# Attention in a ViT tower: the softmax reciprocals spread through DRAM instead of by matmuls, with normalisation and output projection placed later

## What is computed

```
h = concat(cls_tok, edge(x))                       # 32 x 257 x 256
q, k, v = split(layernorm(h) @ w_qkv + b_qkv)      # 16 heads of 16
att = softmax(causal(q @ k.T / 4))
y   = att @ v                                      # heads side by side: 32 x 257 x 256
h   = h + y @ w_out + b_out
h   = h + ffn(layernorm(h))                        # quantised with one scale over all tokens
```

## Time and profile before

| | |
|---|---|
| median of 3 runs | 1192.98 us (1190.79 to 1196.33) |
| the profiled execution: its time | 1186.23 us |
| its span, first to last instruction | 1184.5 us |
| TensorE matmul busy | 960.0 us, 81% |
| VectorE busy | 829.9 us, 70% |
| ScalarE busy | 702.2 us, 59% |
| GpSimd busy | 556.7 us, 47% |
| mean granted TensorE clock | 0.954 of full, 1.00 in the steady part of the attention block |

### The profile page before, as it was taken

How to read it: one execution, slowest core, us unless ns; L and a number is a source line. 1 busy time by engine, 2 the same in 40 slices (tenths; PEclk the granted TensorE clock), 3 DMA queues, 4 the chain that set the end, 5 groups by cost and what they waited for, 6 DMA issues and landing times. The chain is left out here.

```text
span 1184.5 us, 28089 instructions
## 1 busy us (share of the span) xinstructions
PE 960.0 (81%) x9574; PEld 690.6 (58%) x9584; DVE 829.9 (70%) x1967; ACT 702.2 (59%) x1187; POOL 556.7 (47%) x702
## 2 busy tenths in 40 slices
PE   2277899889899989999998989999987478885565
PEld 1055666667676767667676766777765244333343
DVE  1825566777767777776777776767665369998998
ACT  0154556666666666666666666666543167776796
POOL 5233555665566565565556556556543254430000
PEclk9988899999999999999999999999997689997889
DMA  3854555555545655555565555554330024203863
GB/s 88 229 132 114 132 144 135 143 144 149 131 128 148 155 136 149 145 125 136 151 149 140 152 133 128 139 137 116 89 79 13 6 96 194 103 1 103 261 205 108
DMA packets 156102, 152.91 MB, mean 129 GB/s; under 512 B 28263, under 2 KB 152458, under 8 KB 153994
## 3 DMA queue, kind: packets, MB, share of 16 engines
q1 hardware_dynamic: 156042, 152.14, 47.4%
HBM read 67.49 MB, written 28.35 MB: 81 GB/s over the span
## 5 line engine op out<-in xcount | busy, mean ns | idle before, releaser
L542 ACT ACTIVATE prob<-ST 128x772 f32<-128x772 f32 x256 | 209.5, 818 | 150.3 <-PE ST L956 145.3
L706 DVE TENSOR_REDUCE mneg<-SX 128x2 f32<-128x258 f32 x256 | 107.6, 420 | 213.3 <-PE SX L942 212.7
L939 PE MATMUL SX<-kst,qst 96*128 96x257 bf16 (+1 forms) x1024 | 160.2, 250 | 18.3 <-DMA qst<-qpart 8.9
L708 DVE TENSOR_REDUCE mneg<-SX 128x2 f32<-128x514 f32 x256 | 174.1, 680 | 0.0
L956 PE MATMUL ST<-qst,kst 98*128 98x256 bf16 (+2 forms) x1536 | 139.2, 223 | 15.5 <-DMA qst<-mpart 15.2
L451 POOL TENSOR_SCALAR_AFFINE_SELECT prob<-prob 128x1016 f32<-128x1016 f32 x128 | 142.6, 1114 | 0.0
L942 PE MATMUL SX<-mask_s,ident_b 128*128 128x256 bf16 x512 | 142.4, 278 | 0.0
L956 PEld LDWEIGHTS ST<-qst,kst 98*128 98x128 bf16 x1536 | 121.2, 99 | 33.8 <-DMA qst<-mpart 12.0
L975 PE MATMUL G<-prob,vaug 128*32 128x256 f32 (+2 forms) x3072 | 117.4, 282 | 14.5 <-POOL prob L451 13.6
L939 PEld LDWEIGHTS SX<-kst,qst 96*128 96x128 bf16 x1024 | 91.6, 99 | 63.4 <-issue 26.7
L975 PEld LDWEIGHTS G<-prob,vaug 128*32 128x32 f32 x3072 | 83.3, 111 | 48.5 <-POOL prob L451 19.6
(11 more groups left out here) (229 smaller groups left out, 2074.6 us busy)
## 6 DMA issues: line engine op xcount, KB each, us to landing
kst<-kpart SPq DMA_DIRECT2D x192, 128.5 KB, 2.5
xin<-in_x SPq DMA_DIRECT2D x96, 256.0 KB, 4.0
gst<-gray_dram SPq DMA_DIRECT2D x96, 256.0 KB
qst<-qpart SPq DMA_DIRECT2D x192, 128.0 KB, 2.4
h_dram<-hb SPq DMA_DIRECT2D x8, 1280.0 KB, 4.6
gray_dram<-gray SPq DMA_DIRECT2D x64, 128.0 KB, 2.8
result<-xn SPq DMA_DIRECT2D x32, 256.0 KB, 3.7
hb<-h_dram SPq DMA_DIRECT2D x5, 1280.0 KB, 6.5
```

The costliest lines, as they stand in the source:

```text
L542: nc.scalar.activation(prob[:, g % 2, 2 * (u % 2):2 * (u % 2) + 2, 0:QEND], ST[:, :, 0:QEND], ACT.Exp).then_inc(exp_done, 1)
L706: nc.vector.tensor_reduce(mneg[:, 0, u // 4, 0, at], SX[:, :, S0:S0 + P + 1], AX.X, ALU.max, negate=True)
L708: nc.vector.tensor_reduce(mneg[:, 1, u // 4, 0, at], SX[:, :, S1:S1 + T], AX.X, ALU.max, negate=True).then_inc(max_done, 1)
L939: mm(SX[:, r, at:at + k], qst[par][0:SR, 2 * u + r, P * t:P * t + P], kst[par][0:SR, 2 * u + r, 0:k], start=t == 1, stop=False)
```

## The change

- The table `sel`, the tile `rec` and the two matmuls of `spread_rec` are gone. `yn` becomes two tiles that alternate by parity.
- SP stores the reciprocals `den` to a DRAM tensor `rec_dram` of 8 rows of 512 (16 KB), in the place where it moved them into `rec`. After the grey image's stores it waits until that store has landed, and loads `rec_dram` into `yn[par]`: every row 16 times, 128 partitions of 2 KB (256 KB). The loads of the next image and of the grey rows stand behind it.
- VectorE multiplies `yun` by `yn[par]` in place. This instruction now stands after `maxima(bS, 3)` and `edge_tile(bC, 1)`, ahead of `split(bS, 0)`; it stood before `maxima(bS, 3)`. Its second input was a PSUM tile and is now in SBUF.
- The output projection, the residual and the second layernorm of an image come one step later (bR = n-7 instead of bO = n-6), at the same places of the lists; the pipeline has one more step (LAST = 7). 
- `outputs(bT, 2)` no longer waits for `yn_done`.
- ScalarE copies G into `yun` in another order of the four parts, so that `yun` is read contiguously later, and `unnormalised(0)` stands two instructions later, behind `exponential(bT, 7)` and the copy of `qr`.

```
...
-        yn = sb("yn", [P, KC, IMG])
         den = sb("den", [P, H * IMG // P])
-        rec = sb("rec", [H, IMG])
-        sel = sb("sel", [P, 2 * P])
+        yn = [sb(f"yn{i}", [P, KC, IMG]) for i in range(2)]
...
-        LAST = 6
+        LAST = 7
...
                     for j in range(4):
-                        sp.dma_start(yun[32 * j + HD:32 * j + 2 * HD, 0:4:2, :], yun[32 * j:32 * j + HD, 1:4:2, :]
+                        sp.dma_start(yun[32 * j + HD:32 * j + 2 * HD, 0:KC, :], yun[32 * j:32 * j + HD, KC:2 * KC, :]
                                      ).then_inc(y_moved, 16)
                     wait(sp, rec_done, bO, 1, 1)
-                    wait(sp, rec_spread, bO - 1, 1, 1)
-                    sp.dma_start(rec[:, :], den[:, :]).then_inc(rec_moved, 16)
+                    wait(sp, rec_moved, bO - 1, 16, 16)
+                    sp.dma_start(rec_dram.rearrange("r (i c) -> (r i) c", c=H * IMG // P), den[:, :]
+                                 ).then_inc(rec_stored, 16)
...
                         sp.dma_start(gray_dram[1 + P * t:1 + P * t + P, 1:1 + IMG],
                                      gray[:, t, :]).then_inc(gray_saved, 16)
+                if valid(bO):
+                    wait(sp, rec_stored, bO, 16, 16)
+                    wait(sp, out_done, bO - 2, 1, 1)
+                    src = bass.AP(rec_dram.tensor, 0, [[KC * IMG, H // KC], [0, HD], [1, KC * IMG]])
+                    sp.dma_start(yn[par][:, :, :].rearrange("p c t -> p (c t)"), src).then_inc(rec_moved, 16)
                 if valid(n + 1):
                     wait(sp, gray_step, bW, 2, 2)
                     load_x(n + 1, odd)
...
-                        nc.scalar.copy(yun[:, 2 * k:2 * k + 2, :], G[:, k, :].rearrange("p (g t) -> p g t", g=2)
+                        nc.scalar.copy(yun[:, k:4:2, :], G[:, k, :].rearrange("p (g t) -> p g t", g=2)
...
                 queries(1)
-                unnormalised(0)
                 exponential(bT, 7)
                 if valid(bP):
                     wait(act, q_rest, bP, 1, 1)
                     nc.scalar.copy(qpart[:, 1, :, :], qr[:, :, :]).then_inc(q_mid, 1)
+                unnormalised(0)
...
                 edge_tile(bC, 0)
-                if valid(bO):
-                    wait(dve, rec_spread, bO, 1, 1)
-                    wait(dve, y_moved, bO, 64, 64)
-                    wait(dve, out_done, bO - 1, 1, 1)
-                    nc.vector.tensor_tensor(yn[:, :, :], yun[:, 0:4:2, :],
-                                            G[:, 1, :].rearrange("p (c t) -> p c t", c=KC), ALU.mult
-                                            ).then_inc(yn_done, 1)
                 maxima(bS, 3)
                 edge_tile(bC, 1)
+                if valid(bO):
+                    wait(dve, rec_moved, bO, 16, 16)
+                    wait(dve, y_moved, bO, 64, 64)
+                    nc.vector.tensor_tensor(yn[par][:, :, :], yun[:, 0:KC, :], yn[par][:, :, :], ALU.mult
+                                            ).then_inc(yn_done, 1)
                 split(bS, 0)
...
-                if valid(bO):
-                    wait(dve, out_done, bO, 1, 1)
-                    nc.vector.tensor_tensor(h2[:, rows2(bO), :], h2[:, rows2(bO), :],
+                if valid(bR):
+                    wait(dve, out_done, bR, 1, 1)
+                    nc.vector.tensor_tensor(h2[:, rows2(bR), :], h2[:, rows2(bR), :],
...
                         if g % 2 == 0:
                             wait(pe, yun_ready, b - 1, 2, g // 2 + 1)
-                        if g == 2:
-                            wait(pe, yn_done, b - 1, 1, 1)
...
-                def spread_rec():
-                    if valid(bO):
-                        wait(pe, rec_moved, bO, 16, 16)
-                        wait(pe, yun_ready, bO, 2, 2)
-                        for c in range(KC):
-                            last = mm(G[:, 1, IMG * c:IMG * c + IMG], sel[0:H, P * c:P * c + P],
-                                      rec[:, :], start=True, stop=True)
-                        last.then_inc(rec_spread, 1)
-
                 def project(t):
-                    if valid(bO):
+                    if valid(bR):
                         if t == 0:
-                            wait(pe, yn_done, bO, 1, 1)
+                            wait(pe, yn_done, bR, 1, 1)
                             wait(pe, qx_ready, bP, 4, 4)
...
                 scores_t(bT, odd, 5)
-                spread_rec()
                 queries(0)
...
```

More of the change, by code:

```diff
@@ L39 @@
 NB = B * IMG // TB
-C_ID, C_SEL = 0, P
-C_MS = C_SEL + 2 * P
+C_ID = 0
+C_MS = P
 C_BAND = C_MS + P
@@ L57, in shape_constants @@
     c[:, C_MS:C_MS + P] = np.where(np.arange(P) > p, NEG, 0.0)
-    for j in range(4):
-        for g in range(4):
-            first = C_SEL + P * (g // 2) + 32 * j + HD * (g % 2)
-            c[4 * j + g, first:first + HD] = 1.0
     for dy in range(3):
@@ L489, in step @@
                 select(bS, 0)
-                if valid(bO):
-                    wait(pool, ln2, bO, LN, LN)
-                    wait(pool, x2_step, bO - 1, XS, XS)
-                    nc.gpsimd.tensor_tensor(rstd2[:, rows2(bO)], ve2[:, :], half[:, :], ALU.pow
+                if valid(bR):
+                    wait(pool, ln2, bR, LN, LN)
+                    wait(pool, x2_step, bR - 1, XS, XS)
+                    nc.gpsimd.tensor_tensor(rstd2[:, rows2(bR)], ve2[:, :], half[:, :], ALU.pow
                                             ).then_inc(rs2_done, 1)
@@ L833, in step @@
                 maxima(bS, 6)
-                resid_stats(bO)
+                resid_stats(bR)
                 if valid(bP):
@@ L846, in step @@
                 maxima(bS, 7)
-                if valid(bO):
-                    wait(dve, rs2_done, bO, 1, 1)
+                if valid(bR):
+                    wait(dve, rs2_done, bR, 1, 1)
                     for t in range(QT):
-                        nc.vector.tensor_scalar(x2[:, t, :], h2[:, row_of(bO, t), :].rearrange("p o d -> p (o d)"),
-                                                ag2[:, t, 0:1], rstd2[:, row_of(bO, t)],
+                        nc.vector.tensor_scalar(x2[:, t, :], h2[:, row_of(bR, t), :].rearrange("p o d -> p (o d)"),
+                                                ag2[:, t, 0:1], rstd2[:, row_of(bR, t)],
                                                 ALU.subtract, ALU.mult).then_inc(x2_step, 1)
-                    wait(dve, x2_step, bO, XS, 2)
-                    nc.vector.tensor_reduce(colmax[:, rows2(bO)], x2[:, :, :], AX.X, ALU.max,
+                    wait(dve, x2_step, bR, XS, 2)
+                    nc.vector.tensor_reduce(colmax[:, rows2(bR)], x2[:, :, :], AX.X, ALU.max,
                                             apply_absolute_value=True)
-                    nc.vector.tensor_reduce(mean2[:, rows2(bO)], ag2[:, :, 0:1], AX.X, ALU.max).then_inc(x2_step, 2)
+                    nc.vector.tensor_reduce(mean2[:, rows2(bR)], ag2[:, :, 0:1], AX.X, ALU.max).then_inc(x2_step, 2)
                 if isinstance(n, int) and n < 3:
@@ L1074, in transposes @@
                         wait(pe, xhat_done, bC, 2, 2)
-                        wait(pe, ln2, bO, LN, 1)
+                        wait(pe, ln2, bR, LN, 1)
                         if ends:
```

23 lines of the change are left out of this document (11 added, 12 removed).

## The result

The change makes the kernel slower: 1305.47 us (median of 4 runs, 1304.69 to 1307.05) against 1194.65 us for the kernel before in the same session, a ratio of 1.093, 95% interval 1.089 to 1.097. I had forecast 1184 us, and no more than 1204. The mean granted clock of the profiled execution fell from 0.954 to 0.889.

The account below looks back on a forecast made before the run. TensorE was taken as nearly the bound, with chains almost as long as the step. A gain of 0.35 us over 27 steps (9.4 us), other terms together 0, gave 1184 us for the median; range 1167 to 1204.

Parts of the forecast that it names:

- The spread removed: On TensorE, the matmuls spreading the reciprocals go; everything behind comes 1.06 us a step earlier unless another chain holds it.
- The multiply held by GpSimd: On VectorE ahead of `split`, the multiply waits for GpSimd's L471, so the copy of the maxima starts no earlier.
- The select's chain: From GpSimd's L471 and L475 through VectorE's L748 to the select: gains 0.54 us a step instead of 1.06.
- The load hidden from the multiply: The 256 KB load lands before VectorE's multiply can start, or is late by 0.3 us at worst; taken as hidden.
- The 256 KB in front of the placed maxima: On SP's DMA list, the new load issued ahead of the placing of the maxima delays it by 0.
- The other end: The alternative price for the 256 KB delaying the placed maxima: 2.4 us, from a read at 106 GB/s.
- The rule of the skill: DMA engine count follows the pattern's slowest dimension, here 8, so the load runs on half of the 16; no extra cost.
- The clock at 1.00 throughout: TensorE's granted clock, read as 1.00 through the attention block; no loss from a lower clock was priced.
- The third: Rival: nothing is left, as longer query waits or late placed maxima take the gain; about 1193 us, 17%.
- The second: Rival: the load is late, so VectorE stands at the multiply with `split` behind it; 1206 to 1220 us, 15%.
- The rest of the change: Steady steps gain 0.35 us each, 9.4 us over 27 steps; the moved edits cost nothing, the last steps together 0.
- the short chains that it named: Three chains nearly as long as the step: the queries', the select's and the landing of the placed maxima.

Follow-up runs that it names:

- i13: a5 with the multiply moved behind `maxima(bS, 4)`, reciprocals still not multiplied: 1182.1 us, 0.992 of the kernel before.
- a5: a1 with the image loads put back ahead of SP's wait for the store: 1192.1 us, 0.997 of the kernel before.
- a1: The changed kernel with the reciprocals' load cut from 256 KB to 2 KB, the multiply reading only `yun`: 1203.3 us, 1.009 of the kernel before.
- a2: The changed kernel with the same 256 KB load, its slowest dimension 16 instead of 8 (wrong values): 1227.8 us, 1.030 of the kernel before.
- c6: The changed kernel with reciprocals stored twice, load from 16 rows, image loads ahead of SP's wait for the store: 1261.5 us, 1.060 of the kernel before.
- g9: The changed kernel with the 256 KB load from 4 rows, 32 times each (wrong values): 1413.3 us, 1.185 of the kernel before.
- h11: The changed kernel with SP's list reordered: store, grey image, load (8 rows), image loads, then the moves of `yun`: 1221.4 us, 1.021 of the kernel before.
- h12: h11 with the reciprocals stored twice and the load from 16 rows: 1200.5 us, 1.007 of the kernel before.
- i14: h12 with the multiply moved behind `maxima(bS, 4)`: 1209.5 us, 1.014 of the kernel before.
- j17: j16 with the reciprocals stored twice and the load from 16 rows: 1279.9 us, 1.073 of the kernel before.
- j16: The changed kernel with load and multiply in the next step, load behind that step's first placing, ScalarE keeping a copy of `yun`: 1259.3 us, 1.055 of the kernel before.
- b4: The kernel before with an unused 256 KB load (8 rows, 16 times each) added where the change has its load: 1301.7 us, 1.092 of the kernel before.
- k18: j16 with SP's order changed: load, first placing, grey image, image loads, then store and moves: 1188.5 us, 0.996 of the kernel before.
- d8: The changed kernel with the first half's placing issued by ScalarE, load from 16 rows, image loads ahead of SP's wait: 1343.5 us, 1.128 of the kernel before.

## Why the prediction was wrong, point by point

**The spread removed, 1.06 us a step: right.** TensorE closes the gap.

**The multiply held by GpSimd: right.** 1.38 us instead of 0.67 (the median of 32), ending 0.56 us behind L471, and L475, which starts within it, is stretched to 1.40 from 1.17. The copy of the maxima follows the place of the old spread by 6.30 us; I had said 6.5. i13 prices the hold and the place together: with the multiply out of the way, 0.992 instead of a5's 0.997, some 7 us, with intervals that just meet.

**The select's chain: right, and a little more.** From the place of the spread to the end of the select (L451) it was 522.03 - 510.69 = 11.34 us and is 10.50 (L451 at 520.51 for 1.11): 0.84 gained instead of 0.54. L748 still ends with L475, but starts later: 0.47 us at the median instead of 1.12.

**The load hidden from the multiply: right.** In the steady part VectorE never waits for it (three waits in all, 17.9 us, in the last steps). There, with little else in flight, it is 3.6 to 4.2 us from the load's issue to the multiply, and in the very last step 5.2 us from the store's issue, where I had 5.6 to 8.5.

**The 256 KB in front of the placed maxima "priced at 0": wrong, and the whole error.** I argued that a step without image loads has the placing land in 3.28 us against 3.22 with 768 KB of them in front, "so what is issued ahead of the grey rows costs them nothing". The inference runs one way only. It shows that the image loads, begun 7.4 us before the placing, no longer delay it; it does not show that there is room for more. The change used up the room twice: 256 KB more, read over 8 rows, and image loads begun 0.7 us later because SP waits for the store. a1 puts the first at some 100 us, a5 the second at some 10. The second stood in my own list: image loads from 511.7 and the placing still at 517.59 are 5.9 us instead of 7.4, and I didn't price it. The other end that I had written beside the zero, 2.4 us, was not in my range: 27 times 2.4 is 65 us, a time of about 1249 and "slower". Those 2.4 us come from half a microsecond in which the DMA engines were busy for 0.29, so they price no busy queue. The measured size is 3.7 us later to land at the median, and with the clock behind it about 5 us a step, twice my other end.

**The rule of the skill that I cited and waved through** (the load on half of the engines) "would lie inside these bounds": it did for the multiply, the only consumer that I held it against. For the transfer behind it, the layout makes the difference between 1228 us (a2) and 1305.

**The clock at 1.00 throughout: wrong as a consequence.** Over the 400 us of the earlier trace rows it is 0.89 instead of 1.00, and in the step shown it adds about 2 us. The wait need not be 5 us. In a1 a step with a wait of 1.66 us (`scores_t` at 318.72) is granted this:

```profile
318.00:320.00 2.00, 1.28 (x30) 1.03 (x30) 0.72 (x2) 0.62 (x1) 1.55 (x2) 0.99 0.75 206
320.00:322.00 2.00, 2.00 (x25) 1.61 (x14) 0.69 (x2) 1.65 (x5) 0.00 (x0) 0.50 0.77 211
322.00:324.00 2.00, 2.00 (x7) 1.66 (x8) 1.87 (x8) 0.81 (x1) 1.12 (x2) 0.65 0.72 201
324.00:326.00 2.00, 2.00 (x23) 1.75 (x25) 1.38 (x5) 0.69 (x3) 0.83 (x2) 1.00 0.51 138
```

In that run the steps behind placings waited for by up to 1.01 us take 24.8 to 25.3 us, those behind waits of 1.26 to 1.90 take 25.5 to 27.5, and the one behind 3.35 takes 28.8: a wait of half a microsecond more can cost two. That is one run's pattern and no rule: in a5 a step behind a wait of only 0.76 us takes 26.65 us, with the clock at 0.50 from 402 to 404 us, behind three short waits for other things (0.95, 0.32 and 0.22 us, from 398 to 401). So the loss isn't linear in the landing, and pricing a delayed wait at its own length, as I did, leaves out 2.0 of the 6.7 us in the step shown.

**The rivals.** None was this. The third named it ("the placed maxima lie behind the load after all") and priced it at nothing left, 1193. The second came true in c6 and g9 only; in h11 and h12 it was the moves of `yun` that were late, which I had not thought of.

**The rest of the change: about nothing, as forecast to within its own size.** a5, the change without the load's bytes, is at 0.997, 3 us faster (7 faster to 1 slower); I had 9.4 in the steady part. What the spread gives is taken back, as my third rival said, but only in part by the short chains that it named. From 300 to 700 us TensorE waits for 42 us in all, where it was 29 before, most of the growth for the queries (8.1 us, from 1.9) and for L708 (8.9, from none in the list); and the granted clock is 0.97, where it was 1.00. The five shortest steps of a5 take 24.8 to 24.9 us, nearly the whole spread less; the others 25.1 to 27.3.

**What stays open.** Which engines the placing runs on, and so whether it meets the loaded ones or all of them, no record shows. How much of each late landing is owed to the image loads and how much to the grey rows right in front of the placing was not separated: in i14 the image loads begin 7.1 us ahead, and the landing is still 4.9. Why 128 distinct rows are slower than 8 rows read 16 times (1361 against 1305) is not explained. That j17 is slower than j16, though its load is the more even one, goes with its image loads starting later (4.9 against 5.3, for the second store), but wasn't isolated.

## What to carry to other kernels

A transfer that nobody waits for is not free: ask which urgent transfer is issued in the microseconds behind it, and count all the bytes that are still in flight then, this load's and the others', with the layout of each pattern. That taking bytes away changes nothing shows that the queue is just empty in time, and says nothing about adding some; the test is to add a dummy load of the same shape at the same place to the kernel as it is (b4). Spread bulk loads so that they don't stand together in front of an urgent one: k18 has its 256 KB right ahead of a placing, but with the DMA engines otherwise little used (a share of 0.33 from 500 to 503 us and 0.13 from 503 to 505, in the step shown), and its image loads 9.4 us ahead of the next, while j16, with the 256 KB right behind a placing and the image loads late, lost 5.5%. Keep issue waits of small stores out of the way of big loads.

## What the runs showed of the hardware

- The placing of 8 KB takes 2.0 to 10.5 us from issue to use, by what is in flight around it. The medians are 2.4 to 3.4 us in the six kernels before, a5, c6, h11, h12 and k18, in all of which the image loads begin 7.4 us ahead or more. That isn't enough by itself: g9 (load over 4 rows, image loads 8.1 us ahead) has 10.0, d8 (keys in front) 6.3.
- A store of 16 KB to DRAM lands in 1.6 us at the median, less than the 2.8 that I took from 128 KB:

```profile
rec_dram<-den SPq DMA_DIRECT2D x32, 16.0 KB, 1.6
```

- TensorE's granted clock falls to 0.50 of full behind an idle stretch of only 1.66 us, as the rows of a1 above show, and in a5 behind three short ones of 1.49 us together.
